# Four attention layers in one kernel: closer slots for the third layer's scaling and turning, and for the fourth layer's scores and out-projection

## The reference, cut to what matters

```python
x = h + softmax(q k' / sqrt(C)) v            # layer 0, h = group_norm(x); per image 256 x 256 scores
x = gamma1 * (softmax(relu(q) relu(k)') v) + x   # layer 1: each row of 16 positions attends to itself
x = gamma2 * (softmax(q k') v) + x           # layer 2: 256 x 256 scores, 16 channels in q and k
# layer 3: 8 heads of 16 channels, keys and values from a 3x3 average pool with stride 2 (64 positions),
# q, k, v reshaped without a transpose, so that "head" 0 holds the first 32 tokens and 8 keys per channel group
x = out(softmax(q k' / 4) v) @ w_o + b_o + x
```

## Time and profile before

| what | value |
| --- | --- |
| median of 3 runs | 136.36 us (135.73 to 136.48) |
| the profiled execution: its own time, its span | 136.52 us, 134.6 us |
| TensorE busy | 123.1 us, 91% of the span |
| VectorE, ScalarE, GpSimd busy | 62%, 57%, 54% |
| mean granted TensorE clock | 0.975 of full |
| shares of the chain that ended last | PE 73%, DVE 10%, issue 5%, DMA 4% |

### The profile page before, as it was taken

How to read it: one execution, slowest core, us unless ns; L and a number is a source line. 1 busy time by engine, 2 the same in 40 slices (tenths; PEclk the granted TensorE clock), 3 DMA queues, 4 the chain that set the end, 5 groups by cost and what they waited for, 6 DMA issues and landing times.

```text
span 134.6 us, 3603 instructions
## 1 busy us (share of the span) xinstructions
PE 123.1 (91%) x1386; PEld 89.6 (67%) x1386; DVE 83.7 (62%) x196; ACT 76.7 (57%) x228; POOL 73.2 (54%) x120
## 2 busy tenths in 40 slices
PE   6887999989999999999899993999949999999990
PEld 4665799977876777667678871423323775988990
DVE  5776666445324564679779430779699999940081
ACT  0436347788985657576987551333425567597320
POOL 8942616999892123320068888504166666799300
PEclk9999999999999999999999999599995999999999
DMA  3950000000000000000000033424455620000046
GB/s 92 328 172 0 0 5 2 2 0 2 0 5 0 5 0 0 5 0 0 0 0 0 27 102 85 140 83 136 63 70 144 83 22 5 5 0 5 5 124 188
DMA packets 19104, 6.41 MB, mean 48 GB/s; under 512 B 9360, under 2 KB 18960, under 8 KB 19088
## 3 DMA queue, kind: packets, MB, share of 16 engines
q1 hardware_dynamic: 17456, 4.93, 15.5%
q10 hardware_dynamic: 1632, 1.27, 3.2%
HBM read 4.61 MB, written 1.57 MB: 46 GB/s over the span
## 4 chain that ended last, share of the span: by engine, by line
PE 73%; DVE 10%; issue 5%; DMA 4%; POOL 3%; ACT 2%; ACTq 0%; DVEq 0%; POOLq 0%
PE bank L749 11%; PE bank L792 9%; PE bank L694 8%; PE bank L771 8%; PE bank L780 5%; PE bank L713 5%; PE bank L733 5%; DMA x_all<-in_x_dram 4%; PE bank L746 3%; PE bank L685 3%; PE bank L809 3%; PE bank L723 2%; PE bank L760 2%; DVE prob L589 2%; DVE negmax L587 2%
## 5 line engine op out<-in xcount | busy, mean ns | idle before, releaser
L416 ACT ACTIVATE prob<-bank,negmax 128x256 f32<-128x256 f32 (+1 forms) x48 | 19.4, 410 | 14.8 <-DVE negmax L549 10.1
L355 POOL TENSOR_TENSOR prob<-prob,inv 128x512 f32<-128x512 f32 x16 | 16.4, 1044 | 16.0 <-DVE inv L599 16.0
L467 ACT ACTIVATE prob<-prob 128x512 f32<-128x512 f32 x16 | 10.1, 630 | 19.9 <-DVE prob L589 19.9
L771 PE MATMUL bank<-kdiag,qT 128*32 128x512 f32 x128 | 17.4, 666 | 2.2 <-issue 2.2
L749 PE MATMUL bank<-probT,v 128*128 128x256 f32 x64 | 17.1, 389 | 0.7 <-issue 0.7
L694 PE MATMUL bank<-packed,xT 128*128 128x128 f32 (+1 forms) x96 | 15.6, 286 | 0.2 <-ACT prob L416 0.2
L577 DVE SCALAR_TENSOR_TENSOR xT<-bank,packed,xT 128x256 f32<-128x256 f32 x16 | 7.7, 482 | 11.7 <-PE bank L749 6.9
L694 PEld LDWEIGHTS bank<-packed,xT 128*128 128x128 f32 x96 | 13.1, 191 | 1.9 <-issue 1.2
L749 PEld LDWEIGHTS bank<-probT,v 128*128 128x128 f32 x64 | 11.1, 190 | 4.1 <-issue 3.1
L792 PEld LDWEIGHTS bank<-probT,vdiag 128*32 128x32 f32 x512 | 11.7, 113 | 3.0 <-issue 3.0
L587 DVE TENSOR_REDUCE negmax<-bank 128x8 f32<-128x512 f32 x16 | 10.6, 663 | 3.6 <-PE bank L771 3.6
(11 more groups left out here) (102 smaller groups left out, 244.5 us busy)
## 6 DMA issues: line engine op xcount, KB each, us to landing
kdiag<-k_rows SPq DMA_DIRECT2D x32, 64.0 KB, 2.5
out_dram<-x_all SPq DMA_DIRECT2D x8, 128.0 KB, 2.0
x_all<-in_x_dram SPq DMA_DIRECT2D x2, 256.0 KB, 4.1
x_all<-in_x_dram ACTq DMA_DIRECT2D x2, 256.0 KB, 5.5
vdiag<-v_rows SPq DMA_DIRECT2D x8, 64.0 KB, 3.2
packed<-in_pack_dram ACTq DMA_DIRECT2D x1, 321.0 KB, 5.8
k_rows<-kT SPq DMA_DIRECT2D x4, 64.0 KB, 2.1
v_rows<-vt SPq DMA_DIRECT2D x4, 64.0 KB, 2.0
```

The lines of the kernel that those rows point to most:

```text
L355: nc.gpsimd.tensor_tensor(p, p, inv[g][:, t, :].unsqueeze(2).broadcast_to([128, HEADS, KEYS]), ALU.mult)\
L416: last = nc.scalar.activation(prob[g][:, t, 0:keys], psum("scores", layer, g)[:, keys * t:keys * t + keys], ACT.Exp, bias=negmax[g][:, t, ...
L467: nc.scalar.activation(prob[g][:, t, :], prob[g][:, t, :], ACT.Exp).then_inc(s_exp3, 1)
L771: last = mm(ps[STRIP * s:STRIP * s + STRIP, :].rearrange("p (c m k) -> p c k m", c=HEADS, m=HKEY), qT[g][:, 0, HTOK * j:HTOK * j + HTOK], ...
```

## The change

Four distances of the table change. No instruction is added or removed, and no wait is edited.

```diff
-    steps += [("qk", 2, 1), ("v", 2, 1), ("scores", 2, 3), ("scale", 2, 2), ("probT", 2, 2), ("o", 2, 2)]
-    steps += [("pool", 3, 1), ("q", 3, 3), ("kv", 3, 0), ("scores3", 3, 5), ("share3", 3, 2), ("probT3", 3, 2),
-              ("xb", 3, 1), ("pv", 3, 1), ("x", 3, 2), ("y", 3, 6)]
+    steps += [("qk", 2, 1), ("v", 2, 1), ("scores", 2, 3), ("scale", 2, 1), ("probT", 2, 1), ("o", 2, 2)]
+    steps += [("pool", 3, 1), ("q", 3, 3), ("kv", 3, 0), ("scores3", 3, 4), ("share3", 3, 2), ("probT3", 3, 2),
+              ("xb", 3, 1), ("pv", 3, 1), ("x", 3, 2), ("y", 3, 3)]
```

## The result

The changed kernel takes 144.43 us (143.4 to 144.6, 3 runs) and the kernel before 136.36. The ratio is 1.060, 95% interval 1.056 to 1.064: slower by 6%. The forecast was 142.6 with a range of 138.8 to 145.2. The median lies inside that range and just above the narrower one that the forecast called its own (140.2 to 144.2). The profiled execution took 143.4 us with a span of 141.5; the other two had spans of 142.7 and 142.5. One of these had a lower mean clock (0.961 against 0.976); where they lost their last 1 us no trace shows. In what follows, an execution over 1.5% above the fastest of its kernel counts in the median and the range, but not in the ratio.

What follows compares the result with a forecast made beforehand. TensorE, busy in 91% of the span, was taken as the bound, with gains only from its idles and half clock. Terms 3.0 + 3.4 + 0.7 - 0.5 - 0.3 = +6.3, stated as +6.2: 142.6 us, range 138.8 to 145.2.

Steps and rivals of the forecast that it cites:

- Term 1: Layer 2's scaling one slot behind the scores makes the first layer-3 scores later, 82.88 to 85.9: +3.0 us.
- The loop: Layer 2: scaling waits for its exponential, the next exponential for the next maxima, through VectorE and ScalarE; period 2.57 us.
- The pooling's contention: Layer 2: scalings on VectorE run longer beside GpSimd's pooling; 0 to 1.4 us, taken as 0.
- Term 2: Layer 3: keys of pair 3 come late, delaying image 6's scores to 113.0: 6.4 us, 3.4 beyond Term 1.
- D: Layer 3: start of image 1's maxima on VectorE, taken as S + 5.4 us, bounds 4.2 and 6.5.
- S: Start of the first layer-3 scores on TensorE, forecast at 85.9 us.
- The clock: TensorE at image 6's scores: an idle ahead brings half clock; +0.7 us, bounds 0 and 1.6.
- the allowance of -0.5 for hidden waits: TensorE's 24.9 us from image 6's scores on: short waits hidden in merged rows given back, between 0 and 1.0 us.
- The out-projections: End of the kernel: three out-projections go earlier, so the last output DMA has no queue before it; -0.3 us.
- The two single causes: Rivals: only layer 2's loop costs, about 139.2 us, 15%; only the keys of pair 3 cost, about 139.7, 10%.
- more than forecast: Rival: contention with the pooling (1.4) and low clock at both TensorE gaps (0.9), about 144.8 us; 14%.
- The faster one: Rival: layer 2's loop hides and keys 3 arrive in time, 135.2 us; 6%.

Runs made afterwards that it cites:

- the fourth run: Changed kernel, but VectorE keeps the order of before in layer 2 (maxima of the next image ahead of the scaling): 142.03 us, ratio 1.044 to the kernel before.
- the sixth run: Changed kernel, but ScalarE copies the keys of pairs 2 and 3 ahead of the exponentials of images 1 and 3: 140.13 us, ratio 1.033 to the kernel before.
- the first run: Kernel before with only the layer-2 distances of scale and probT at 1: 139.53 us, ratio 1.026.
- the third run: Kernel before with only the out-projection distance at 3: 135.54 us, ratio 0.997.
- the first of the last four versions: Kernel before with out-projection at 3 and ScalarE copying keys of pairs 2 and 3 ahead of the exponentials of images 0 and 2: 133.91 us, ratio 0.985.

## Why the prediction was right, and where its sizes were off

**Term 1, +3.0; measured +3.2.** The loop was as described and its period as worked out, shown by VectorE's order alone (2.58 and 2.57). In the changed kernel it is slower, 2.78, outside the 2.5 to 2.7 that were to be the sign. I gave TensorE's part 0.45 in all, and the eighth maxima, laid at 75.38, came at 76.16: 1.23 above the bare loop and beyond the bound of 0.9. Three of the six periods are long, 3.02, 2.98 and 2.91, and the others are 2.58 or 2.59. The first has the wait at 62.52: TensorE's scores of images 2 and 3 stand behind a transpose and a bank which exponential 1 frees. The second has the like wait at 68.09, for the scores of images 4 and 5. The third has the late residual add at 69.63 with a scaling of 0.92 behind it. That TensorE's queue closes a loop of its own I did not see; it took the miss of the fourth run to find it. The keys' copy, laid at 77.38, was at 78.15, and the chain from it to the first scores took 7.91 and not 8.49 (the keys' write landed sooner). That the two errors nearly cancel is luck.

**The pooling's contention, 0 to 1.4, taken as 0.** Of layer 2's eight scalings five run beside pooling, four of them within the loop. One in the loop took 0.92 (70.16), and so did the fifth, outside it, at 79.39; the sum's term was 0.23 at most. The rule of the Trainium skill (GPSIMD Engine Reference, the table at its head) is that GpSimd contends with VectorE instructions such as these scalings. I read it as all of them being long, and the kernel before as bearing it out in half of the cases. That reading was too narrow: where the scaling kept its 0.69, the pooling instruction beside it was the long one (last section). Taking near 0 was right.

**Term 2, +3.4 beyond term 1; measured +2.7.** The mechanism held: late copies by ScalarE's order (the sixth run, 4.1 us of the distance), an idle ahead of image 6's scores with no releaser named, gone when only layer 2 changes (the first run). Three sizes inside were off and offset each other. D was laid at S + 5.4 and was S + 3.8 (86.06 to 89.84), below its lower bound of 4.2. The clock did not fall behind the first idle, and VectorE's first maxima were followed by D without a gap (87.18 to 89.84). That idle was 1.94 us in place of the 4 us forecast, since TensorE's own work of layer 2 ended 3.4 us later as well (80.72 before, 84.12 now). The way from D to SP's write was laid at 12.95 and took 13.00 (to 102.84). SP then began placing after 2.27 and not 3.1. From the first placing DMA to the scores it took 7.34 (105.11 to 112.45), and not 5.56, of which the issuing alone is 5.36 in place of 3.65. Sum of the three: -1.6 - 0.8 + 1.8 = -0.6. The forecast of 3.4 owes its nearness to that. Why these eight DMAs are slow to issue stays open: without values ahead of them it was 4.70, and 3.91 in the execution with TensorE kept busy.

**The clock, +0.7, and the allowance of -0.5 for hidden waits; measured +1.27 together.** Of the terms of the sum these two together were the furthest off. The low stretch fell wholly on image 6's scores (3.38, against 1.92), 1.45 by the runs without it, and the work behind it took 24.7 us at full clock, so the allowance is 0.2 and not 0.5. Ahead of images 4 and 6 an idle was followed by half clock, ahead of image 0 it was not: those scores took 1.92. The rule of the Trainium skill (TensorE: Matmul & The Clock Gate, Part 1), half clock after idleness, held for two of the three.

**The out-projections, -0.3; measured -0.26 in the span** and 0.6 by medians of the third run, whose interval reaches to 0.

**The median.** The profiled execution came 0.7 above my 142.7. The median came 1.8 above my 142.6, because here the profiled execution was the fastest of three, and in the kernel before slower than the other three. So the profiles account for 6.9 of the 8.1 us. What the rest is no trace shows.

**The sum's edges.** With the bounds of the text the upper sum is 145.9, or 147.2 with the pooling's 1.4, and not 146.4. The lower sum leaves out 0.5 of the allowance and 0.3 of the output queue, with which it is 138.7. Two rivals are priced 0.1 off by their own terms (139.1 and 144.9). None of this moves the forecast.

**The rivals.** The two single causes are each real (139.5 and 140.7 us when made alone) but neither is alone. The nearest to the measured median is "more than forecast", 144.8. Its clock part nearly came true (1.45, where it had 1.6), its contention part did not (0.23 at most, of 1.4), and what lifts the median there is the unexplained 1 us. So the nearness is mostly luck. The faster one needed both conditions, and both failed: the eighth exponential at 76.88 and not 73.1, keys 3 written at 102.84 and not 98. Its kernel of truth was the wait at the values' copy: the version that takes it away in the kernel before, with the closer out-projection, is the one at 133.91.

## What to carry to other kernels

Before a step is moved closer to the one it depends on, write down for each queue what then stands between producer and consumer. Where nothing is left, the round trip through both engines becomes the period. Summed from four rows it came out within 0.01 us where it stood alone (2.58), and 0.2 short where TensorE's waits joined in (2.78). More than one queue that walks the same order can close such a loop, so undoing it in one may not be enough. A small copy that starts a DMA chain belongs ahead of the long-waiting work of its engine: that move on ScalarE, with the closer out-projection, gave 1.5%, of which the out-projection alone gave 0.3%. Larger distances with the closer out-projection gave 0.8% and 0.6%.

## What the runs showed of the hardware that was not expected

The clock does not fall after every idle of about 2 us. It stayed up behind idles of 1.94 us at 84 to 86 (changed kernel), 3.19 us ahead of image 6's scores (SP placing keys 3 first), and 2.12 us followed by several shorter ones (VectorE's order alone, full clock throughout); it fell behind idles of 2.01 us (the first of the last four versions, first scores 3.38 us), 2.15 and 3.11 us. Why it fell after some and not after others stays open. Issuing the same eight placing DMAs took from 3.62 to 5.36 us on SP.

Where a scaling of layer 2 on VectorE and a pooling instruction on GpSimd overlapped by more than 0.1 us, in either kernel, the one of the two that started later ran long. In the changed kernel:

```profile
70.16 0.92 DVE L560 TENSOR_TENSOR prob<-prob,inv 128x512 f32<-128x512 f32 x1
...
72.97 0.69 DVE L560 TENSOR_TENSOR prob<-prob,inv 128x512 f32<-128x512 f32 x1
```

```profile
70.13 0.40 POOL L367 TENSOR_TENSOR prob<-xT 128x128 f32<-128x128 f32 x1 [0.89 <-DVE xT L580]
...
72.98 0.98 POOL L369 TENSOR_TENSOR prob<-prob,xT 128x112 f32<-128x112 f32 x1
...
82.21 0.44 POOL L369 TENSOR_TENSOR prob<-prob,xT 128x112 f32<-128x112 f32 x1
```

At 70.16 the scaling came 0.03 us behind the pooling instruction and took 0.92 in place of 0.69. At 72.97 it came 0.01 ahead, kept its 0.69, and the pooling instruction took 0.98 in place of the 0.44 that it takes alone (82.21).
